# Linear attention of a GNN block: the context taken from the value weights alone, attention per pair of tiles with features on partitions, and one mixing product per tile

## The reference, cut to what matters

```python
q = x @ Wq.T
k = x @ Wk.T
v = x @ Wv.T
q = softmax(q, axis=-1) * dim ** (-0.5)
k = softmax(k, axis=-2)
context = einsum('bnd,bne->bde', k, v)
attn = einsum('bnd,bde->bne', q, context)
x = attn + x
return x @ W1.T @ W2.T + x
```

## Time and profile before

| | us |
|---|---|
| median of 3 runs | 462.78 |
| the profiled execution's own time | 462.53 |
| its span in the profile | 460.8 |
| PE busy (share of the span) | 447.6 (97%) |
| DVE busy | 324.0 (70%) |
| ACT busy | 149.7 (32%) |
| granted PE clock | 0.999 |

### The profile page before, as it was taken

One profiled execution on the slowest core, in us unless ns is written; L12 is line 12 of the kernel. 1 busy time (PEld: TensorE's weight loads), 2 busy tenths in 40 slices (PEclk: granted clock), 3 DMA queues, 4 the chain that ended last, 5 costly groups with the idle time before them and its releaser, 6 DMA issues.

```text
span 460.8 us, 6803 instructions
## 1 busy us (share of the span) xinstructions
PE 447.6 (97%) x2405; PEld 358.5 (78%) x2405; DVE 324.0 (70%) x1106; ACT 149.7 (32%) x271; POOL 66.1 (14%) x91
## 2 busy tenths in 40 slices
PE   8999999999999999999999999999999998888996
PEld 5777788888888888887889999877777766655783
DVE  5988699879988988898971110444645666777972
ACT  3666574304223222351232110222132114551120
POOL 5414700000000000000004000002200000007652
PEclk9999999999999999999999999999999999999999
DMA  8930200390000000003000000002744449305891
GB/s 248 261 93 2 91 0 1 93 222 23 2 1 1 1 1 1 0 3 119 10 1 4 1 1 1 1 0 84 269 134 132 131 134 382 140 2 182 301 368 66
DMA packets 20414, 40.44 MB, mean 88 GB/s; under 512 B 2521, under 2 KB 2851, under 8 KB 20373
## 3 DMA queue, kind: packets, MB, share of 16 engines
q1 hardware_dynamic: 18117, 32.53, 23.3%
q0 software_dynamic: 2256, 7.39, 4.5%
HBM read 30.09 MB, written 10.31 MB: 88 GB/s over the span
## 4 chain that ended last, share of the span: by engine, by line
PE 83%; DVE 9%; ACT 3%; issue 2%; DMA 1%; SPq 0%; POOLq 0%; POOL 0%; DVEq 0%
PE ps L756 41%; PE ps L1074 9%; PE ps L996 9%; PE ps L883 6%; PE ps L743 5%; PE ps L937 2%; ACT scrap_a L1477 1%; DMA RAW_A<-in_mW 1%; PE ps L1091 1%; PE ps L1180 1%; PE ps L913 1%; DVE stat L1532 1%; PE ps L1023 1%; DVE XTL L1561 1%; PE ps L1210 1%
## 5 line engine op out<-in xcount | busy, mean ns | idle before, releaser
L1786 DVE TENSOR_SCALAR RING_D<-places,PLACES 125x170 bf16<-125x170 f16 x260 | 67.7, 260 | 0.0
L1787 DVE TENSOR_SCALAR RING_S<-iota,HOME 125x128 bf16<-125x128 f16 x260 | 64.2, 247 | 0.0
L996 PE MATMUL ps<-AT,H1H 125*128 125x416 f32 (+1 forms) x108 | 38.0, 352 | 0.2 <-issue 0.2
L996 PE MATMUL ps<-AT,H1L 125*128 125x416 f32 (+1 forms) x108 | 38.0, 351 | 0.0
L1074 PE MATMUL ps<-H2H,AT 125*125 125x512 f32 x90 | 36.1, 402 | 0.0
L1074 PE MATMUL ps<-H2L,AT 125*125 125x512 f32 x90 | 35.5, 394 | 0.0
L1091 PE MATMUL ps<-WE0H 128*128 128x512 f32 x129 | 35.4, 407 | 0.0
L1928 DVE SCALAR_TENSOR_TENSOR ZL<-ps,ZH 128x416 fp32r<-128x416 f32 (+1 forms) x12 | 6.3, 584 | 39.1 <-ACT ZH L1419 39.1
L621 POOL TENSOR_TENSOR G2L<-RAW_G,G2H 128x512 fp32r<-128x512 f32 x4 | 5.0, 1291 | 186.5 <-ACT G2H L1229 186.5
L1849 DVE TENSOR_TENSOR ps<-ps,bias 125x512 f32<-125x512 f32 x20 | 14.0, 700 | 20.8 <-PE ps L756 20.8
L743 PEld LDWEIGHTS ps<-RING_D,RING_S 125*125 125x125 bf16 x260 | 24.1, 136 | 5.4
(11 more groups left out here) (413 smaller groups left out, 1159.6 us busy)
## 6 DMA issues: line engine op xcount, KB each, us to landing
RAW_E<-in_experts SPq DMA_DIRECT2D x8, 1024.0 KB, 10.1
RAW_AGAIN<-in_experts SPq DMA_DIRECT2D x3, 1024.0 KB
X<-in_x SPq DMA_DIRECT2D x1, 2240.0 KB
out_x<-X SPq DMA_DIRECT2D x10, 224.0 KB
scratch<-X SPq DMA_DIRECT2D x10, 224.0 KB
scratch<-Y SPq DMA_DIRECT2D x10, 224.0 KB
RAW<-in_mW2T SPq DMA_DIRECT2D x4, 256.0 KB, 4.3
RAW_A<-in_mW SPq DMA_DIRECT2D x4, 256.0 KB, 4.8
```

What stands on the lines that cost most here:

```text
L996: pe.matmul(place(f), h[0:TT, k, 128 * f:128 * (f + 1)], AT[0:TT, k, c0:c1], start=(k == 0 and n == 0), stop=False)
L1786: V.tensor_scalar(hot_d(v, width(b)), places[0:ET, 0:width(b)], PLACES[0:ET, c:c + 1], None, ALU.is_equal)
L1787: V.tensor_scalar(hot_s(v), iota[0:ET, :], HOME[0:ET, c:c + 1], None, ALU.is_equal).then_inc(done["marked"], 1)
```

## The change

- **Context.** `vp` goes. `cp` is now T · Wv with the split value weights themselves, so CP holds the context, not the context times MP. Wq is loaded and split first, Wv second, and the graph's W1 goes to another buffer, loaded once `q9` is done.
- **Early queries.** `q0` and `q1` take the place of `vp` in step 3 with the transposes of `KMAX` ahead of the eighth product of `q0` and `kmb` ahead of the fifth of `q1`. Their exponentials, sums and transposes move into step 4. The diagonal matrices are built by ACT, after a copy of the identity. Within the context the low half of exp(k) is used last, and most additions to `ESUM` come after the ninth low half.
- **Attention by pairs.** `attend(p)` gives (attn + x)ᵀ of tiles 2p and 2p+1: for each of four feature blocks two products of an identity with x's halves and 12 of CP's block (stationary) with the transposed queries, all with 2 x 126 = 252 columns. ACT and DVE split the result to SH and SL.
- **One mixing product.** `mix(i)` is 12 products of S with MP.
- **Visits.** 39 groups in place of 48, most of 9 or 10; DVE's marks are ordered anew.

The diff, cut:

```diff
-    for c in range(C):
-        use(f"vp{c}", (4, 5, 6), ("vph_ready", c + 1), ("vpl_ready", c + 1))
...
+    use("q0", (4,), ("rmax_ready", 1), ("q_exp", 1))
+    use("kmt", (7,), ("kmt_ready", 1))
+    use("q1", (6,), ("rmax_ready", 2), ("q_exp", 2))
+    use("kmb", (7,), ("k_shift", NT))
...
-def visits_in_products(long):
-    spots = [("cp", n, 3) for n in range(0, 48, 6)]
...
+def visits_in_products():
+    spots = [("cp", n, 4) for n in range(12, 48, 6)]
+    for p in range(PAIRS):
+        a, b = 2 * p + 2, 2 * p + 3
+        if a < NT:
+            spots += [(f"q{a}", 6, 9 if p else 5)]
+        spots += [(f"a{p}", 28, 10)]
+        if b < NT:
+            spots += [(f"q{b}", 6, 9), (f"x{a - 2}", 6, 9), (f"x{b - 2}", 6, 10 if p else 9)]
+        else:
+            spots += [(f"x{a - 2}", 0, 5), (f"x{a - 2}", 6, 5), (f"x{b - 2}", 6, 9)]
     for i in range(NT - 1):
-        spots += [(f"h{i}", 0, 3), (f"h{i}", 6, 3)]
+        spots += [(f"h{i}", 6, 6 if i else 7)]
...
             sp.wait_ge(done["cpl_ready"], C)
             sp.dma_start(bias[0][0:TT, :], gb1.rearrange("(a f) -> a f", a=1).broadcast_to([TT, D])).then_inc(loads["b1"], 16)
+            reads(sp, f"q{NT - 1}")
+            load_weight("g1", gW1T)
...
+            tile_product("q0", 0, WQH, WQL, between=turn_peaks, at=7)
+            tile_product("q1", 1, WQH, WQL, between=peak_rows, at=4)
...
+            def attend(p):
+
+                for h in range(2):
+                    ps = opens(f"at{p}_{h}")
+                    visits(f"a{p}", 28 * h)
+                    for k in range(2):
+                        f = 2 * h + k
+                        block = slice(128 * f, 128 * (f + 1))
+                        o = ps[:, 2 * (TT + 1) * k:2 * (TT + 1) * (k + 1)]
+                        for n, x in enumerate((XTH, XTL)):
+                            pe.matmul(o, identr[:], x[:, 2 * p:2 * p + 2, f, 0:TT + 1], start=(n == 0), stop=False, skip_group_check=True)
+                        if f == 0:
+                            pe.wait_ge(done["qtl_ready"], 2 * p + 2)
+                            if p == 0:
+                                pe.wait_ge(done["cpl_ready"], C)
+                        for c in range(C):
+                            for n, (w, q) in enumerate(((CPH, QTH), (CPH, QTL), (CPL, QTH))):
+                                mm = pe.matmul(o, w[:, c, block], q[:, c].rearrange("p t n -> p (t n)"), start=False, stop=(c == C - 1 and n == 2), skip_group_check=True)
+                    closes(f"at{p}_{h}", mm)
...
             def mix(i):
-                ps = opens(f"xq{i}")[0:TT, :]
-                terms(ps, (tile_of(XTH, i), tile_of(XTL, i)), (rows_of(MPH), rows_of(MPL)), last=False, unit=f"x{i}")
-                visits(f"x{i}", 12)
...
+                p, t = i // 2, i % 2
+                product(f"xq{i}", opens(f"xq{i}")[0:TT, :], (lambda c: SH[:, c, t, 0:TT], lambda c: SL[:, c, t, 0:TT]), (rows_of(MPH), rows_of(MPL)),
+                        before=lambda c: pe.wait_ge(done["sl_ready"], 2 * p + c // 2 + 1), unit=f"x{i}")
...
+            for p in range(PAIRS):
+                a, b = 2 * p + 2, 2 * p + 3
+                if a < NT:
+                    tile_product(f"q{a}", a, WQH, WQL, unit=f"q{a}")
+                attend(p)
+                if b < NT:
+                    tile_product(f"q{b}", b, WQH, WQL, unit=f"q{b}")
+                for i in (2 * p, 2 * p + 1):
+                    mix(i)
+                    if i + 2 < NT:
+                        turn_q(i + 2)
...
+            act.wait_ge(done["kmt_ready"], 1)
+            copy(identr[:], ident[:])
             for c in range(C):
-                reads(act, f"vp{c}")
-                copy(VPH[:, c, :], ps_of(f"vp{c}")[:]).then_inc(done["vph_ready"], 1)
...
+                ins = copy(diag[:, c, :], ident[:], scale=kmt[:, c:c + 1])
+            ins.then_inc(done["diag_ready"], 1)
...
+            chosen_keys()
+            for i in range(3, NT - 2):
+                add_exp(i)
             add_exp(NT - 2)
             add_exp(NT - 1)
...
+            mark_next(RING_A)
...
+            for p in range(PAIRS):
+                a, b = 2 * p + 2, 2 * p + 3
+                mark_next(5)
+                if a < NT:
+                    q_peak(a)
                 else:
+                    split_lo("g1", 0)
+                    split_lo("g1", 1)
+                mark_to(f"a{p}")
+                if a < NT:
+                    q_inverse(a)
+                mark_next(3)
+                attn_left(p, 0)
+                if b < NT:
+                    mark_to(f"q{b}")
+                else:
+                    split_lo("g1", 2)
+                    split_lo("g1", 3)
+                attn_left(p, 1)
+                if b < NT:
+                    mark_next(4)
+                    q_peak(b)
+                mark_to(f"x{a - 2}")
+                if b < NT:
+                    q_inverse(b)
+                mark_next(4)
+                add_mix(a - 2)
+                if b < NT:
+                    q_left(a)
+                mark_to(f"x{b - 2}")
+                mark_next(4)
+                add_mix(b - 2)
+                if b < NT:
+                    q_left(b)
+                mark_to(f"q{a + 2}" if a + 2 < NT else f"a{p + 1}" if b < NT else "h0")
```

More of the change, by code:

```diff
@@ L114, in psum_plan @@
     use("ranks", (5,), ("tiles_step", 3))
+    for i in range(2):
+        use(f"qt{i}", (4,), ("qth_ready", i + 1), ("qtl_ready", i + 1))
     use("homes", (6,), ("home_ready", 1))
@@ L537, in _ @@
             sp.dma_start(ROWS[0:TP], rows_in).then_inc(loads["edges"], 16)
[L538 removed]
+            for last, name, w in (("w1", "wq", WqT), ("wq", "wv", WvT)):
                 sp.wait_ge(*hi_of(last, C - 1))
@@ L846, in _ @@
             for c in range(C):
[L847 to L851, removed]
+                pe.wait_ge(*lo_of("wq", c))
+            tile_product("q0", 0, WQH, WQL, between=turn_peaks, at=7)
+            tile_product("q1", 1, WQH, WQL, between=peak_rows, at=4)
             def tile_ranks():
@@ L874, in chosen_tiles, with context @@
                 closes("keys", mm)
[L876 to L880, removed]
+            def context(i, c, first=0, last=3):
+                ps = opens(f"tt{c}") if i == 0 and first == 0 else PS[plan[f"tt{c}"][0]]
                 f = slice(128 * c, 128 * (c + 1))
-                for n, (x, e) in enumerate(((XNH, EH), (XNH, EL), (XNL, EH))):
+                for n, (x, e) in list(enumerate(((XNH, EH), (XNL, EH), (XNH, EL))))[first:last]:
+                    if n == 0:
+                        pe.wait_ge(done["xnl_ready"], i + 1)
+                        pe.wait_ge(done["eh_ready"], i + 1)
+                    if n == 2:
+                        pe.wait_ge(done["el_ready"], i + 1)
                     mm = pe.matmul(ps[:], x[0:TT, i, f], e[0:TT, i % 4, :], start=(i == 0 and n == 0),
@@ L886, in context, with turn_q @@
                     closes(f"tt{c}", mm)
-                elif c == C - 1:
+                elif c == C - 1 and last == 3:
                     mm.then_inc(done["e_used"], 1)
-            for i in range(NT - 2):
+            def turn_q(i):
+                pe.wait_ge(done["q_ready"], i + 1)
+                opens(f"qt{i}")
+                for c in range(C):
+                    mm = pe.transpose(view(f"qt{i}")[:, c, 0:TT], Q[0:TT, i % 2, 128 * c:128 * (c + 1)], ident[0:TT, 0:TT])
+                closes(f"qt{i}", mm)
+            for first, last in ((0, 2), (2, 3)):
+                for c in range(C):
+                    context(0, c, first, last)
+            for i in range(1, NT - 2):
                 for c in range(C):
                     context(i, c)
-                if i == 1:
+                if i == 3:
                     tile_ranks()
-                if i == 6:
+                if i in (4, 5):
+                    turn_q(i - 4)
+                if i == 7:
                     chosen_tiles()
```

316 lines of the change are left out of this document (142 added, 174 removed).

## The result

The changed kernel takes **482.83 us** (median of 4 runs, 481.68 to 484.49), the kernel before beside it 462.86 (462.64 to 463.08): a ratio of 1.0434, with an interval of 1.0401 to 1.0467. The direction is the one forecast. The size is not: 475.3 was forecast, with a range that ended at 482. The profiled execution took 481.68 us with a span of 479.9.

A forecast was written before the change was run, and what follows sets the result against it. PE's work alone was taken to bound the kernel before, with DVE nearly full; 462.53 - 2.3 (front) - 0.5 (PE's loop work) + 15.3 (new waits) = 475.0, or 475.3 for the median; range 459 to 482.

The forecast's parts named there:

- PE's own work in the loop: From `cp` to the big product with the counts: products, visits and transposes removed and added change PE's work by -0.5 us.
- What bounds the kernel: Loop over tiles: PE's work alone sets the time before, DVE staying ahead; the walk ends at 243.0 against 243.10.
- The products: Attention by pairs: 280 products of 252 columns at 0.122 us add 34.2 us; 38.8 us of other products go.
- The rival of 0.188: Attention's narrow products cost 0.188 us each, bound by the loader: 18.5 us more, 493.8 us; chance 0.07.
- The new waits: Loop: PE waits for marks behind DVE's waits, 3.6 us a pair; the walk's sum is +15.3 us.
- DVE stays ahead: Rival, loop: no new waits, only the first two terms count, 460.0 us, or 458.7 if additions are not late; chance 0.20.
- half the waits: Rival, loop: PE's small slips let DVE catch up in part, 467.7 us; chance 0.07.
- The front: Before `cp`: context starts at about 57.95, column sums at 88.0, `cp` at 90.1 instead of 92.4, -2.3 us.
- the front gains nothing: Rival, before `cp`: additions or ACT's diagonals end late, 477.6 us; inside the forecast's own range, no separate chance.
- The additions: End of the context on DVE: 7 additions behind `chosen_keys`, 7 x 0.61, run from 82.5 to 87.2.
- The chance of 0.80 for slower: Whole kernel: probability that the change makes it slower; faster had 0.17, same 0.03.

The follow-up runs named there:

- the run with half marks: Changed kernel with the second one-hot matrix of a mark no longer written once the ring is full (counts left wrong): 473.02 us, ratio 1.0218 to the kernel before.
- the ring of seven: Kernel before with the ring of one-hot matrices cut from 16 to 7 slots, nothing else: 476.00 us, ratio 1.0257.
- the first run: Changed kernel with `q_left(0)`, the low half of the first transposed query, read two tiles earlier on DVE: 476.62 us, ratio 1.0287 to the kernel before.
- mended front: Changed kernel with `q_left(0)` after tile 6, three late additions before the edge keys' wait, two low halves of T before the first six marks: 474.20 us, ratio 1.0236.

## Why the prediction was right and wrong

**The sum, term by term**, from 462.53 to 481.68, both profiled executions:

| | forecast | measured |
|---|---|---|
| start of `cp` (front) | -2.3 | +4.0 |
| first products of `cp` at half clock | 0 | +1.6 (4.42 for twelve, not 2.78) |
| PE's own work in the loop, at 0.122 | -0.5 | -0.5 (not read by itself) |
| narrow products at 0.117, not 0.122 | 0 | -1.4 |
| new waits | +15.3 | +15.3 or so (what remains of 15.1; read directly, 13.7 in the groups of visits and 1.3 at the last attention, 214.20 - 212.77 less the 0.12 of a product) |

- **What bounds the kernel**: right. From `cp` to the big product the forecast had 255.6 - 90.1 = 165.5, and the changed kernel takes 165.77. That it is so near is partly luck: 1.6 us of half clock were missing in it, and the narrow products were 1.4 too dear.
- **The products**: right, and 0.005 too dear each. The ends were 0.110 and 0.188; the line through 512 and 416 columns was the right guide. The rival of 0.188 is out, and with it the rule of the Trainium skill ("TensorE: Matmul & The Clock Gate", where it stands in the section "The mechanism") that a load overlaps a matmul only where the row groups differ. By it the narrow product would have cost an estimated 0.21; the starts stand 0.117 apart. This case's trace contradicts it at 252 columns too.
- **The new waits**: right in size, place and cause. Written: 0.65, 1.6 and 1.3 a pair and a pair every 26.1 us; measured: 0.69, 1.62 and 1.29, and the attentions of three pairs start at 140.27, 166.13 and 192.03, 25.9 apart. The run with more marks ahead of each wait removes 11.0 of it without removing an instruction, which shows that it is the marks behind the waits; the run with half marks removes 10.0. The last attention's wait, written as 1.4, is there with 1.3 (1.16 in the profile's own count of idle time).
- **The rivals "DVE stays ahead" and "half the waits"** are out. It was right to read the order and not the busy share; the ring of seven shows in the kernel before too that DVE's lead, and not its load, decides.
- **The front: this step failed.** The first part held: the context was to start at 57.95 and starts at 57.71. Then the forecast said that PE reaches the column sums at 88.0 and named no wait on the way; of the early queries it counted only the exponentials, as "hidden in ACT's gaps under the context". I had priced the transposes of both queries (0.9) as work and had not asked what each of them waits for. The second set waits for the bank of the first, which DVE empties at tile nine, at 78.48, while PE is there at 75.4. That costs 3.8, and the half-clock products behind it in the context 1.6 more (3.66 and not 2.05 to the eighth); the first run removes both, and `cp` starts 5.1 sooner. The rival "the front gains nothing" looked for the loss in the additions and the diagonals and ended at 0; it had not this wait either.
- **The additions**: the step "7 additions, 7 x 0.61" was a size off. They took 5.37 to the next operation's start, and 4.27 was forecast: 1.1 us. In the chain they stand (5.46 - 0.68) / 6 = 0.80 apart, with 0.68 as the reported duration of one, and the earlier trace rows had it: (2.27 - 0.68) / 2 = 0.80. I took the price of a single operation for a chain of them.
- **Nothing of the forecast had the clock in it.** The kernel before had a granted clock of 0.999, and I carried full clock over to a kernel in which PE stands still. The first products of `cp` at 0.43 cost 1.6 us. The mended front, with the short waits only, has 1.00 in the same window.

Had the front been priced with these three, the forecast of the profiled execution would have been 475.0 + 6.3 + 1.6 = 482.9 (6.3 is the front's 4.0 for -2.3), or 481.5 with the narrow products at their measured price, against 481.68. The chance of 0.80 for slower stood on the loop alone and was justified by it; the front, which was to give 2.3 us, took 5.6, and the range had 0 as its dear end there. That end was my choice without a bound from above: a wait that the trace of before cannot show was given no price at all.

## What to carry to other kernels

When two in-order engines meet at many places, write out the order of both with the distances between starts, and price every wait. The busy share says nothing of it: here PE waited 15 us for an engine that was 83% busy in the window shown. Count for each group what has been made *ahead* of the last wait before it; making the groups larger without moving the producer's work forward turns a lead into a lag, and moving a few numbers gives it back. And for every instruction that is moved or newly placed, ask what frees its bank, not only what feeds it.

## What the runs showed of the hardware

- **A wait of PE can cost more than its length, and not every wait does.** After 3.78 us of standing still, products of 512 columns stood 0.43 apart instead of 0.23 (half of full speed, the level of 1.2 GHz) for six products; after 2.45 us, in the run with more marks ahead, sixteen products of 252 columns stood 0.21 apart instead of 0.117. At the start of `cp`, behind eight products of one column and a wait of 1.67, the changed kernel has eight distances of 0.43, and the run with `q_left(0)` early has all twelve products slow (5.26 us). The runs with more marks ahead and with half marks have the first three distances as at full clock and then seven of 0.43. After waits of 1.05, 1.16 and 1.48 with full work before them, the products went on 0.23 or 0.117 apart. Whether the wait or the one-column products decide at `cp` is open; the mended front kept these products, lost the wait, and ran at full clock.
- **The times scatter by more than 2 us, whatever the kernel.** The four runs of the changed kernel lie within 2.8 us and the four of before beside them within 0.4, but eleven later runs of the kernel before lie between 462.40 and 465.26. In the profiled run of the ring of seven, 2.5 us are lost before the ring is used at all: its context starts at 64.95 instead of 62.48. Why is open.
- **Additions in a chain into one tile start 0.80 apart on DVE**, a single one between other operations costs 0.61. Seven take 5.46; four in the mended front take 3.07, again (3.07 - 0.68) / 3 = 0.80. That the dependence is the reason is argued only.
- **A product of 252 columns costs 0.117**, less than the line through 416 and 512 columns gave, although its weight load is reported with 0.188.
